# A planned transformer layer on one core: global attention units issued in pairs, six prob buffers, a finer bias product and a new plan

## The reference

```
x = x + layernorm(attn(layernorm(x)))       attn: x += global(rmsnorm(x)); x += local(rmsnorm(x))
x = x + layernorm(ffn(layernorm(x)))        ffn: shared expert + 1 of 8 routed experts, ternary weights
global: 16 heads of 8, 4 key/value heads, rope, q and k normalised per head, causal softmax
local:  the same with a band mask: 0 <= i - j < 32
```

## Time and profile before

| | |
|---|---|
| median of 3 runs | 707.4 us (706.96 to 707.48) |
| the profiled execution | 709.0 us, its span 707.3 us |
| TensorE busy, share of the span | 77% |
| VectorE, ScalarE, GpSimd busy | 57%, 50%, 33% |
| mean granted TensorE clock | 0.904 of 2.4 GHz |

### The profile page before, as it was taken

One profiled execution on the slowest core, in us unless ns is written; L12 is line 12 of the kernel. 1 busy time (PEld: TensorE's weight loads), 2 busy tenths in 40 slices (PEclk: granted clock), 3 DMA queues, 4 the chain that ended last, 5 costly groups with the idle time before them and its releaser, 6 DMA issues.

```text
span 707.3 us, 15690 instructions
## 1 busy us (share of the span) xinstructions
PE 542.5 (77%) x5734; PEld 268.9 (38%) x5749; DVE 404.9 (57%) x1054; ACT 354.2 (50%) x490; POOL 234.5 (33%) x624
## 2 busy tenths in 40 slices
PE   1226649868896989889988989889999999538354
PEld 1204225424453443544444454344335343434242
DVE  2663966455476575757665566545535642654665
ACT  1021326854663578447846765666696678004010
POOL 3524784275256226411560211401110331050100
PEclk9956568997998999999999999999999999679666
DMA  8000000000000000000000000000000000000000
GB/s 233 1 0 1 1 2 1 2 1 1 2 3 1 1 10 1 2 1 9 1 2 2 8 3 1 9 2 2 9 1 2 1 10 2 1 0 2 7 0 8
DMA packets 8809, 6.17 MB, mean 9 GB/s; under 512 B 1944, under 2 KB 8096, under 8 KB 8736
## 3 DMA queue, kind: packets, MB, share of 16 engines
q10 hardware_dynamic: 3424, 2.64, 1.3%
q1 hardware_dynamic: 5312, 2.52, 1.3%
HBM read 4.11 MB, written 1.05 MB: 7 GB/s over the span
## 4 chain that ended last, share of the span: by engine, by line
PE 42%; DVE 23%; POOL 18%; issue 10%; ACT 5%; DVEq 1%; SPq 0%; DMA 0%; POOLq 0%; ACTq 0%
PE osum_g L900 11%; PE scores L874 8%; PE misc L1008 5%; ACT prob L733 5%; PE misc L997 4%; PE scores L868 3%; PE misc L900 3%; POOL qe_l L657 2%; POOL ke_l L662 2%; DVE early L1319 2%; DVE qT L1213 2%; PE misc L850 1%; PE misc L936 1%; PE misc L841 1%; DVE early L1360 1%
## 5 line engine op out<-in xcount | busy, mean ns | idle before, releaser
L733 ACT ACTIVATE prob<-scores 128x1024 f32<-128x1024 f32 (+3 forms) x352 | 307.5, 931 | 177.0 <-PE scores L874 174.2
L900 PE MATMUL osum_g<-prob,V 128*32 128x256 f32 (+1 forms) x2304 | 173.8, 392 | 12.0 <-ACT oTs_g L742 4.4
L874 PE MATMUL scores<-qT,kT 64*128 64x512 bf16 (+3 forms) x760 | 128.2, 358 | 26.9 <-ACT prob L733 13.3
L673 POOL TENSOR_SCALAR_AFFINE_SELECT prob<-prob 128x512 f32<-128x512 f32 x64 | 40.9, 660 | 140.1 <-ACT prob L733 139.9
L874 PEld LDWEIGHTS scores<-qT,kT 64*128 64x128 bf16 x760 | 34.9, 93 | 136.2 <-issue 121.9
L900 PEld LDWEIGHTS osum_g<-prob,V 128*32 128x32 f32 x2304 | 52.4, 111 | 75.8 <-issue 56.7
L1008 PE MATMUL misc<-t2T,h1p 128*128 128x512 bf16 x177 | 46.2, 414 | 10.6 <-DVE h1p L1353 5.8
L690 POOL TENSOR_SCALAR frs<-fmv 128x1 f32<-128x1 f32 x16 | 3.7, 229 | 149.6 <-DVE fmv L1376 149.4
L997 PE MATMUL misc<-early,t1T 128*128 128x256 bf16 x384 | 47.5, 285 | 1.0 <-DVEq L1322 0.6
L1360 DVE TENSOR_TENSOR early<-misc,oh 128x512 f32<-128x512 f32 x32 | 22.0, 687 | 37.3 <-PE misc L1008 36.4
L997 PEld LDWEIGHTS misc<-early,t1T 128*128 128x128 bf16 x384 | 38.2, 102 | 10.4 <-issue 3.6
(11 more groups left out here) (210 smaller groups left out, 794.1 us busy)
## 6 DMA issues: line engine op xcount, KB each, us to landing
X<-in_L_attn_hidden_dram SPq DMA_DIRECT2D x8, 128.0 KB, 4.7
early<-in_L_ffn_expert_w_dram ACTq DMA_DIRECT2D x1, 1024.0 KB, 7.6
out_dram<-X SPq DMA_DIRECT2D x16, 64.0 KB, 1.5
rope<-in_rope_dram SPq DMA_DIRECT2D x1, 256.0 KB, 3.4
early<-in_L_ffn_shared_w_dram ACTq DMA_DIRECT2D x2, 128.0 KB, 8.0
wraw_l<-in_L_attn_l_wq_dram ACTq DMA_DIRECT2D x1, 64.0 KB, 2.5
ident<-in_ident_dram SPq DMA_DIRECT2D x1, 64.0 KB, 2.4
wraw_g<-in_L_attn_g_wq_dram SPq DMA_DIRECT2D x1, 64.0 KB
```

The costliest lines, as they stand in the source:

```text
L673: pool.affine_select(out=d, in_=d, compare_op=ALU.is_ge, fill=0.0, base=0, pattern=[[0, 4], [1, P]], channel_multiplier=-1).then_inc(mask_ ...
L733: act.activation(prob[:, n % NP, :, lo:hi], src, ACT.Exp, scale=float(HD) ** -0.5).then_inc(exp_done, 1)
L874: ins = pe.matmul(o[:, :, c:c + w], kT[a][rows, g, P * (t % kept[a]):P * (t % kept[a]) + P], qT[a][rows, b % Q_KEPT[a], 2 * g:2 * g + 2, q ...
L900: ins = pe.matmul(o[32 * m:32 * m + 32, q:q + w], V[a][:, t % kept[a], g, :], prob[:, n % NP, j, c:c + w], start=(first and k == 0), stop= ...
```

## The change

Four things. The plan now takes global units two at a time: two `qk` in a row, and the two `pv` of a pair in a row. `NP` goes from 5 to 6 prob buffers. The band mask of a local unit, a matmul of 128 columns of the identity, is written as four of 32 columns each. And for two fronts (global block 0 and local block 7) the second `expand` goes from GpSimd to VectorE, so that the two run side by side. The table of step times and the bonuses are new as well, which reorders the whole plan.

```
-NP = 5
+NP = 6
...
+SHARED = [(G, 0, 1), (L, NB - 1, 1)]
...
-    "fw1": [(PE, 3.404)], "fz": [(DVE, 0.614)], ...  "fw2": [(PE, 5.916)],
+    "fw1": [(PE, 5.223)], "fz": [(DVE, 0.544)], ...  "fw2": [(PE, 12.348)],
...
+    if s[0] == "expand" and s[1:] in SHARED:
+        return [(DVE, 1.8)]
...
-        if blocks and room() and len(late) < NP - 1:
+        if blocks and room(2) and len(late) < NP - 2:
...
-            if left[(b, g)] > 1 or not b or ("oT", G, b - 1, 1) in plan:
+            if left[(b, g)] > 2 or not b or ("oT", G, b - 1, 1) in plan:
                 for u in late:
-                    if u[1:3] == (b, g):
+                    if u[1:3] == (b, g) and u == pair_of(u)[0]:
                         options.append((tried(("pv", *u), ended[u])[0] - PULL["pv"], "pv", u))
...
+            for _ in range(2):
+                b, at = blocks.pop(0)
+                put(("qk", G, b, *at), 0.0)
+                late.append((G, b, *at))
...
+            for u in pair_of(what):
+                late.remove(u)
+                t = put(("pv", *u), ended[u])
+                left[u[1:3]] -= 1
...
-                        pe.matmul(o[:, :, lo:end], identb[:], bias.unsqueeze(1).broadcast_to([P, 2, end - lo]),
-                                  start=True, stop=False, skip_group_check=True)
+                        for k in range(4):
+                            pe.matmul(o[32 * k:32 * k + 32, :, lo:end], identb[:, 32 * k:32 * k + 32],
+                                      bias.unsqueeze(1).broadcast_to([P, 2, end - lo]), start=True, stop=False,
+                                      skip_group_check=True)
...
+            def expand(a, b, i):
+
+                if (a, b, i) not in SHARED:
+                    return
+                dve.wait_ge(part_ready[a], b + 1)
...
+                for p, (lo, n) in enumerate([(0, 3), (3, 3), (6, 2)]):
+                    src = part[a][:, p, i, 0:P].rearrange("p (h d) -> p h d", d=HD)
+                    dve.tensor_copy(qe[a][:, i, :, lo:lo + n, :], src.unsqueeze(2).broadcast_to([P, H, n, HD]))
```

More of the change, by code:

```diff
@@ L115 @@
+    "frouter": [(PE, 0.313), (ACT_E, 0.1), (DVE, 2.286)], "fparts": [(DVE, 1.471)],
     "fohT": [(PE, 0.223), (DVE, 1.031)], "fmask": [(PE, 0.647), (DVE, 2.0)], "fw1s": [(PE, 0.624), (DVE, 0.998)],
-    "fw1": [(PE, 3.404)], "fz": [(DVE, 0.614)], "fact": [(ACT_E, 1.229)], "fh1": [(DVE, 3.219)], "fw2": [(PE, 5.916)],
-    "fsel": [(DVE, 2.299)], "fw2s": [(PE, 0.614)], "fsum": [(DVE, 1.218), (POOL, 1.433)], "fout": [(DVE, 0.884)],
-}
-HOP = 0.537
-STALL_PE, STALL_OTHER = 0.98, 0.432
-KNOBS = {"fronts": 2, "feed": 30.371}
+    "fw1": [(PE, 5.223)], "fz": [(DVE, 0.544)], "fact": [(ACT_E, 1.023)], "fh1": [(DVE, 2.39)], "fw2": [(PE, 12.348)],
@@ L125 @@
+    "fsel": [(DVE, 2.299)], "fw2s": [(PE, 0.998)], "fsum": [(DVE, 1.218), (POOL, 1.433)], "fout": [(DVE, 1.017)],
+}
+HOP = 0.803
+STALL_PE, STALL_OTHER = 1.231, 0.432
+LATE = {"close": 0.0, "local": 0.5, "attend": 0.5, "norms": 0.5, "feed": 0.0}
+KNOBS = {
+    "fronts": 2, "feed": 30.371,
+}
 PULL = {
-    "pv": -0.5, "close": 0.66, "local": 0.9, "attend": 0.931, "norms": 1.43, "feed": 0.0, "front": 0.5, "qk": 0.0,
-    "evac": 0.3,
+    "pv": -0.5, "close": 0.988, "local": 0.9, "attend": 0.169, "norms": 0.447, "feed": 0.0, "front": 0.5, "qk": 0.0,
+    "evac": 1.307,
@@ L282, in advance, with pair_of @@
                 to.steps += steps
+    def pair_of(u):
+        us = [(G, u[1], *x) for x in units_of(G, u[1])]
+        k = us.index(u) // 2 * 2
+        return us[k:k + 2]
     put(("weights",), 0.0)
```

38 lines of the change are left out of this document (21 added, 17 removed).

## The result

The changed kernel takes 705.89 us (median of 20 runs, 700.41 to 708.41) where the kernel before, on the same chip, took 708.82 us (median of 20, 706.66 to 715.32). The ratio of the two, taken round by round, is 0.9943, 95% interval 0.9922 to 0.9965. So the change is worth 3 us by the medians and 4 by the ratio, where 21 were forecast, with 674 us as the low end and 703 us as the high end. The profiled execution has a span of 704.1 us against 707.3.

The account below looks back on a forecast made before the run. TensorE was taken to bound the middle (240 to 604 us), chains of small steps the start and end. Terms of -10 + 0 - 3 - 8 = -21 from 707.4 us gave 686.4 us, 8-in-10 range 674 to 703 us.

Parts of the forecast that it names:

- Term 1: Middle stage, 240 to 604 us: pairing score products and products with V gains 10 us, bounds 0 and 21.
- rival C: In score pairs: the wait for the exponential eats the saving, slower, 717 us; decides from 0.22 us a pair; chance 0.08.
- The prediction's own sign: Middle stage: TensorE's waits for the exponential would be above 9.2 us but below 25; near 40, rival C holds.
- term 4: End, after the last global `wo`: reordered steps and a parallel expansion gain 8 us, bounds 2 and 11.
- the prediction's last sentence: Middle stage: the forecast would be wrong altogether if TensorE's clock were lower than 0.99, its idle moments being fewer but longer.
- Term 2: Local units' band product in four groups of 32 columns: 0 us, bounds 4 us faster and 3 us slower.
- Rival E: Local units' band product: 32-column weight loads go one after another, 49 us lost, 735 us in all; chance 0.02.
- Term 3: Start: first scores at about 58 us, block 2's keys copied at 98; 3 us gained, bounds 8 gained and 11 lost.

## Why the prediction was wrong

**Term 1 failed, first at the step "Not all of it is time [...] I take 10, since TensorE is busy 91% of the stage".** The price was right (21.4 us counted, 21.6 measured off TensorE's busy time). What becomes of it was mis-sized. The step took 7 us off for the exponentials in bare stretches and 4 for other stalls. With half exponentials the 21.6 us give 14.6 us of the middle, so 7 go into stalls that have nothing to do with whole exponentials; with whole ones 3.9 us are left, so the exponentials take about 11. In all the pairs bring 5 to 7 us by the ratios, where 10 were taken. The mechanism lies in the two score buffers: the second score product of a pair needs the exponential of the second one of the pair ahead, and while TensorE is busy elsewhere ScalarE has at most two exponentials to do and then stands still; it can't work ahead. That the waiting is for the exponentials is shown; that a third buffer would end it is not, no run has one. The slots show where this hurts. The cover by other work was largely right: such pairs wait 0.19 us each, and 7.1 of their 11.2 us stay with half exponentials. The bare pairs wait 0.56 us each where the step had 0.29, and 16.9 us become 3.5 with half exponentials. The 0.92 us an exponential that the step used holds none of ScalarE's other work (`oevac`, tanh); that this makes the difference is not shown. It was rival C's mechanism, at 0.32 us a pair in the mean and above its point of 0.22. Its sum of 717 us was wrong nonetheless, since it took the waits as added to the time of before; they are paid out of the saving, of which they leave a fifth to a quarter. The prediction's own sign, TensorE's waits for the exponential between 9.2 and 25 us, was met with 14.7 and told nothing, since the waits inside merged rows are not in that figure.

**The sum also had no term for what the new order does to the middle.** It put this at nothing and gave no reason, though the table and the bonuses reorder the whole plan. With 105 pairs taken apart on TensorE alone the middle is 8.2 us longer than before, and 6.2 with half exponentials. By these profiles it is the larger miss, 8.2 us against the 6 by which the pairs fell short, and it turns their gain into a middle 4.3 us longer. 2.4 us of it are the end's work done earlier (term 4). For the other 6 the traces point to the clock, as the prediction's last sentence said it might be: 37.9 us at half clock in the middle against 13.7 before, and at 0.34 us each the 24 us more make 8 us, enough for it. But this price is taken from executions that differ in the clock and perhaps in more, and single profiles of one program differ by 3.6 us in this stage. And why the clock falls oftener stays open. The half-clock stretches of the middle come with holes in TensorE's work around them, such as the 3.82 us at 436.17, and then clock and hole both lengthen the stage; what each is worth was not told apart. With half exponentials the clock is as low (37.5 us), so the wait inside the pair isn't what lowers it. An order with fewer holes was not found.

**Term 2 was right**: 0 us taken, and 0.9995 (0.9973 to 1.0017) measured. Rival E, the loads one after another, is out. The Trainium skill (TensorEngine Tiling (Array Packing), Restrictions) says that column tiling disables Fast Weight Load. No run here shows whether it was off, but the measurement decides on the cost, which is none in this place.

**Term 3 was nearly right in its mechanism, and off by 2.8 us in size.** The timelines of the changed kernel for VectorE and TensorE, to set beside the earlier trace rows:

```profile
54.30 0.68 DVE L1241 COPY kT<-misc 128x1024 bf16<-128x1024 bf16 x1
...
91.82 0.68 DVE L1241 COPY kT<-misc 128x1024 bf16<-128x1024 bf16 x1
```

```profile
56.77 0.82 PE L896 MATMUL scores<-qT,kT 64*128 64x512 bf16 x4 [5.20 <-DVEq L1255]
```

First scores at 56.8 where about 58 was said, the keys of block 2 copied at 91.8 where 98 was, and all of the 10 us made up by 240 us. But block 3's keys, for which the prediction allowed a wait, came 5.5 us later than before (118.9 against 113.4 on TensorE), and of 3 us gained 0.2 were left.

**Term 4 was right in its stage, -8 said and -8.1 measured**, and from the last global to the last local `wo` it is 46.6 us where some 46 was said. The timelines of the changed kernel on VectorE, GpSimd and TensorE, to set beside the earlier trace rows:

```profile
631.88 1.18 DVE L1227 COPY qe_l<-part_l 128x384 bf16<-128x384 bf16 x3
632.97 0.67 DVE L1231 COPY ke_l<-part_l 128x96 bf16<-128x96 bf16 x3
```

```profile
631.93 1.42 POOL L677 TENSOR_SCALAR qe_l<-part_l 128x384 bf16<-128x384 bf16 x3 [2.39 <-DVE part_l L1215]
```

```profile
655.05 0.44 PE L947 MATMUL misc<-ident,on_l 128*128 128x128 f32 x2 [1.30 <-DVEq L1269]
655.95 0.71 PE L958 MATMUL misc<-wo_l,onT_l 128*128 128x128 f32 x4 [0.46 <-ACT onT_l L767]
```

The two halves of the expansion run side by side, VectorE's in 1.8 us where 1.7 was taken, and `onT` waits for no `fw2`. But the first local scores come 34.4 us after `wo` where 33.5 was said, and a stage can be shortened by moving its work ahead of the line at which it is cut. The term took 1 us for the expert masks that now stand ahead of the last global `wo`; 2.4 us of the 8.1 came back in the middle, and on the old plan 7.8 of 9.9. With that work put back the end gains 2.6 us (100.3 against 102.9) and not 8, so the exact hit is partly luck.

## What to carry to other kernels

Saved work on a busy engine is time only if the engine that takes over can run ahead; count the buffers between the two before the share of busy time, and look for waits in merged rows that name none. A new order is a change of its own and needs a term of its own. Test one engine's order by changing that engine's order alone: a shared list, or a constant that the planner reads too, moves everything. And when a gain is found behind a milestone, look what has been moved ahead of it.

## What the runs showed of the hardware

At half clock a group of 16 products with V takes 1.51 us (588.46) or 1.94 us (438.57) where it takes 1.07 at the full one. Over a whole stage a microsecond at half clock costs less than this: 0.34 to 0.4 us in the middle, where TensorE is busy nine tenths of the time, and 0.14 us over the whole execution. Two executions of the same program had 27.3 and 37.9 us at half clock in the same stage and differed by 5.8 us in span (698.3 and 704.1), which is more than the change brought: a single profile can't tell a change of this size.
